# First attention: single-precision probabilities and values, one product for each head

## The reference, cut to what matters

```python
def _L0_xattn_ref(q, k, v, W_q, W_k, W_v, W_o, b_o):      # q: 32x128x128, k = v: 32x77x128
    H = 16; D_K = 8
    qh = jnp.einsum('bsd,hdk->hbsk', q, W_q)
    kh = jnp.einsum('bsd,hdk->hbsk', k, W_k)
    vh = jnp.einsum('bsd,hdk->hbsk', v, W_v)
    scores = jnp.einsum('hbsk,hbtk->hbst', qh, kh) / jnp.sqrt(D_K)
    attn = jax.nn.softmax(scores, axis=-1)
    out = jnp.einsum('hbst,hbtk->hbsk', attn, vh)
    out = jnp.transpose(out, (1, 2, 0, 3)).reshape(q.shape[0], q.shape[1], H * D_K)
    return out @ W_o.T + b_o
...
x = x + jnp.tanh(g_xattn[0]) * _L0_xattn_ref(_layernorm(x, axis=-1), ctx_1024, ctx_1024, ...)
```

## Time and profile before

| | |
|---|---|
| median of 3 runs | 1363.77 us (1361.43 to 1364.35) |
| profiled execution | 1359.99 us, its span 1358.2 us |
| TensorE busy / its weight loads | 1036.5 us / 814.9 us |
| VectorE / ScalarE / GpSimd busy | 874.3 / 859.2 / 889.6 us |
| mean granted clock of TensorE | 0.846 |
| first attention | about 135 to 303 us of the span, granted clock 0.50 from 137 us on |

### The profile page before, as it was taken

One profiled execution on the slowest core, in us unless ns is written; L12 is line 12 of the kernel. 1 busy time (PEld: TensorE's weight loads), 2 busy tenths in 40 slices (PEclk: granted clock), 3 DMA queues, 4 the chain that ended last, 5 costly groups with the idle time before them and its releaser, 6 DMA issues. The chain is left out here.

```text
span 1358.2 us, 36485 instructions
## 1 busy us (share of the span) xinstructions
PE 1036.5 (76%) x13317; PEld 814.9 (60%) x13317; DVE 874.3 (64%) x2471; ACT 859.2 (63%) x1791; POOL 889.6 (65%) x1065
## 2 busy tenths in 40 slices
PE   1568999967894499999999999899999920566660
PEld 1445777753552278887777778777777820355550
DVE  5788788876877766666666656566665611344445
ACT  0568899964663478888877778787777810233330
POOL 1160899964767456677788888888888976144441
PEclk9869555558996599999999999999999965888985
DMA  9993000000221001112112121211212111322215
GB/s 219 261 283 85 10 16 17 16 16 12 44 43 28 1 17 34 32 28 43 33 37 50 31 59 33 53 33 38 52 34 53 33 48 48 56 58 60 63 45 187
DMA packets 210051, 78.40 MB, mean 58 GB/s; under 512 B 149663, under 2 KB 206154, under 8 KB 209883
## 3 DMA queue, kind: packets, MB, share of 16 engines
q1 hardware_dynamic: 179467, 61.91, 21.1%
q10 hardware_dynamic: 25872, 5.56, 2.3%
q0 software_dynamic: 4544, 8.67, 2.0%
HBM read 14.15 MB, written 30.47 MB: 33 GB/s over the span
## 5 line engine op out<-in xcount | busy, mean ns | idle before, releaser
L1671 DVE TENSOR_REDUCE attention_negmax<-bank 128x2 f16<-128x410 f32 x256 | 137.7, 579 | 166.3 <-PE bank L1423 164.4
L1223 POOL TENSOR_TENSOR attention_pl_l<-attention_probs_l,attention_ph_l 128x512 f16<-128x512 f32 x128 | 148.3, 1159 | 97.3 <-ACT attention_ph_l L1552 95.6
L636 POOL TENSOR_TENSOR attention_probs_l<-attention_probs,attention_probs_h 77x512 f16<-77x512 f32 x128 | 145.3, 1152 | 52.8 <-ACT attention_probs_h L718 48.5
L1223 POOL TENSOR_TENSOR attention_pl_c<-attention_probs_c,attention_ph_c 77x512 f16<-77x512 f32 x128 | 147.8, 1154 | 0.0
L1984 POOL DMA_INDIRECT outputs<-experts_y_rows,experts_ids x78 | 77.5, 994 | 102.4 <-ACT experts_y_rows L1921 87.3
L1406 PE MATMUL bank<-layer_kv,ah 128*128 128x128 f16 x1024 | 108.7, 220 | 11.7 <-PEq L2062 11.5
L1438 PEld LDWEIGHTS bank<-identh,attention_negmax 128*128 128x128 f16 (+1 forms) x1024 | 83.3, 107 | 55.9 <-issue 0.3
L1452 PE MATMUL bank<-attention_vh_l,attention_ph_l 128*128 128x65 f16 x512 | 96.0, 195 | 18.2 <-POOL attention_pl_c L1223 18.2
L1406 PE MATMUL bank<-v1h,layer_kv 128*128 128x256 f16 (+1 forms) x512 | 106.4, 275 | 1.3 <-DVE attention_vl_c L1678 1.3
L1665 DVE SCALAR_TENSOR_TENSOR attention_tl<-bank,attention_th 128x512 f16<-128x512 f32 x128 | 87.8, 686 | 28.8 <-ACT attention_th L1543 28.7
L1552 ACT ACTIVATE attention_probs_l<-bank 128x512 f32<-128x512 f32 x128 | 76.2, 595 | 38.3 <-PE bank L1438 36.4
(11 more groups left out here) (367 smaller groups left out, 4150.1 us busy)
## 6 DMA issues: line engine op xcount, KB each, us to landing
tokens<-blank SPq DMA_DIRECT2D x1, 18360.0 KB, 71.0
experts_both<-outputs SPq DMA_DIRECT2D x8, 512.0 KB, 5.2
X<-in_x SPq DMA_DIRECT2D x4, 512.0 KB, 9.4
attention_pay<-attention_pay SPq DMA_DIRECT2D x8, 256.0 KB, 2.8
out<-X ACTq DMA_DIRECT2D x8, 256.0 KB, 4.3
attention_turned_h<-attention_heads_h SPq DMA_TRANSPOSE x96, 2.2
attention_turned_l<-attention_heads_l SPq DMA_TRANSPOSE x96, 2.4
outputs<-experts_y_rows,experts_ids POOLq DMA_INDIRECT x78
```

The source lines that it names most:

```text
L636: pool.tensor_tensor(probs_l[:, n % SLOTS], probs[:, n % 2], probs_h[:, n % SLOTS], ALU.subtract).then_inc(p_split, 1)
L1223: last = pool.tensor_tensor(low[:, g % 2], whole[:, g % 2], high[:, g % 2], ALU.subtract)
L1671: last = dve.tensor_reduce(negmax[:, g, 2 * i:2 * i + 2], score[i], AX.X, ALU.max, negate=True)
```

## The change

Probabilities stay in single precision: ScalarE takes one exponential of each unit into one of 8 single-precision buffers. GpSimd's program in attention0 is gone, with the buffers of high and low parts. Values are kept in single precision too, 9 numbers for each sample and head, written by ScalarE alone, which now releases the bank; VectorE's low half and its setting of the zeros are gone. TensorE makes one single-precision product for each head (77 x 128 stationary, 77 x 9 moving), and waits for exped in place of p_split. The sum of halves is gone: reciprocal and multiplication read the PSUM bank themselves, and TensorE waits for normed in place of totalled before it writes the bank again.

```diff
@@ project0, ScalarE
-                        last = act.activation(vals[:, one, :, 0, 0:DK0], head, ACT.Copy, scale=1.0 / WS)
-                    last.then_inc(v_hi, 1)
+                        last = act.activation(vals[:, one, :, 0:DK0], head, ACT.Copy, scale=1.0 / WS)
+                    last.then_inc(v_out, 1)
@@ project0, VectorE
-            for i, value in enumerate((1.0, 0.0)):
-                dve.memset(vals[:, :, :, i, DK0:DK0 + 1], value)
+            dve.memset(vals[:, :, :, DK0:DK0 + 1], 1.0)
...
-                    dve.wait_ge(v_hi, i * 2 + (u + 1))
-                    for c in range(CH):
...
-                        last = dve.scalar_tensor_tensor(vals[:, one, :, 1, 0:DK0], head, 1.0 / WS, vals[:, one, :, 0, 0:DK0],
-                                                        ALU.mult, ALU.subtract)
-                    last.then_inc(v_out, 1)
@@ attention0
-        probs = m.sb("probs", [C, 2, HG, S])
-        probs_h, probs_l = m.sb("probs_h", [C, SLOTS, HG, S], FP16), m.sb("probs_l", [C, SLOTS, HG, S], FP16)
+        probs = m.sb("probs", [C, SLOTS, HG, S])
...
-        mix = bank[6][:, 0:H * 2 * (DK0 + 1)].rearrange("p (h i k) -> p h i k", i=2, k=DK0 + 1)
+        mix = bank[6][:, 0:H * (DK0 + 1)].rearrange("p (h k) -> p h k", k=DK0 + 1)
...
-        @block.gpsimd
-        def _(pool):
-            for n in range(B * G):
-                pool.wait_ge(exped, n + 1)
-                if n >= SLOTS:
-                    pool.wait_ge(mixed, n - SLOTS + 1)
-                pool.tensor_tensor(probs_l[:, n % SLOTS], probs[:, n % 2], probs_h[:, n % SLOTS], ALU.subtract).then_inc(p_split, 1)
@@ attention0, TensorE
-                    pe.wait_ge(p_split, n + 1)
+                    pe.wait_ge(exped, n + 1)
                     if j == 0 and b:
-                        pe.wait_ge(totalled, b)
+                        pe.wait_ge(normed, b)
                     for i in range(HG):
                         v = HG * j + i
-                        pe.matmul(mix[:, v], probs_h[:, n % SLOTS, i], vals[:, b, v], start=True, stop=False)
-                        last = pe.matmul(mix[:, v, 0], probs_l[:, n % SLOTS, i], vals[:, b, v, 0], start=False, stop=True)
+                        last = pe.matmul(mix[:, v], probs[:, n % SLOTS, i], vals[:, b, v], start=True, stop=True)
@@ attention0, ScalarE
-                if n >= 2:
-                    act.wait_ge(p_split, n - 1)
                 if n >= SLOTS:
                     act.wait_ge(mixed, n - SLOTS + 1)
-                act.activation(probs[:, n % 2], score_t[n % 4], ACT.Exp)
-                act.activation(probs_h[:, n % SLOTS], score_t[n % 4], ACT.Exp).then_inc(exped, 1)
+                act.activation(probs[:, n % SLOTS], score_t[n % 4], ACT.Exp).then_inc(exped, 1)
@@ attention0, VectorE
-                dve.tensor_reduce(summed[:], mix.rearrange("p h i k -> p h k i"), AX.X, ALU.add).then_inc(totalled, 1)
-                dve.wait_ge(totalled, b + 1)
-                dve.reciprocal(recip[:], summed[:, :, DK0]).then_inc(inverted, 1)
+                dve.reciprocal(recip[:], mix[:, :, DK0]).then_inc(inverted, 1)
                 dve.wait_ge(inverted, b + 1)
-                dve.tensor_tensor(heads_out[:, b % 2], summed[:, :, 0:DK0], recip[:].unsqueeze(2).broadcast_to([S, H, DK0]),
+                dve.tensor_tensor(heads_out[:, b % 2], mix[:, :, 0:DK0], recip[:].unsqueeze(2).broadcast_to([S, H, DK0]),
                                   ALU.mult).then_inc(normed, 1)
```

More of the change, by code:

```diff
@@ L507, in project0 @@
         q_high, k_high = m.sb("q_high", [128, 2, CH, S], FP16), m.sb("k_high", [128, 2, CH, C], FP16)
-        q_done, q_hi, q_lo, k_done, k_hi, k_lo, v_done, v_hi, v_out, biased = (
-            m.sem(n) for n in ("q_done", "q_hi", "q_lo", "k_done", "k_hi", "k_lo", "v_done", "v_hi", "v_out", "biased"))
+        q_done, q_hi, q_lo, k_done, k_hi, k_lo, v_done, v_out, biased = (
+            m.sem(n) for n in ("q_done", "q_hi", "q_lo", "k_done", "k_hi", "k_lo", "v_done", "v_out", "biased"))
         block = m.block()
@@ L579, in _ @@
                                                  1.0 / WS, k_high[:, g % 2], ALU.mult, ALU.subtract).then_inc(k_lo, 1)
-                    dve.wait_ge(v_hi, i * 2 + (u + 1))
-                    for c in range(CH):
-                        one = bass.ds(i * (2 * CH) + (CH * u + c), 1)
-                        head = v_bank[u][:, D * c:D * c + D].rearrange("p (o h k) -> p o h k", o=1, k=DK0)
-                        last = dve.scalar_tensor_tensor(vals[:, one, :, 1, 0:DK0], head, 1.0 / WS, vals[:, one, :, 0, 0:DK0],
-                                                        ALU.mult, ALU.subtract)
-                    last.then_inc(v_out, 1)
         @block.gpsimd
@@ L603, in attention0 @@
         negmax = m.sb("negmax", [S, G, HG], FP16)
-        probs = m.sb("probs", [C, 2, HG, S])
-        probs_h, probs_l = m.sb("probs_h", [C, SLOTS, HG, S], FP16), m.sb("probs_l", [C, SLOTS, HG, S], FP16)
-        summed, recip, heads_out = m.sb("summed", [S, H, DK0 + 1]), m.sb("recip", [S, H]), m.sb("heads_out", [S, 2, H, DK0])
+        probs = m.sb("probs", [C, SLOTS, HG, S])
+        recip, heads_out = m.sb("recip", [S, H]), m.sb("heads_out", [S, 2, H, DK0])
         heads_h, heads_l = m.sb("heads_h", [S, 2, D], FP16), m.sb("heads_l", [S, 2, D], FP16)
@@ L609, in attention0 @@
         bn = m.sb("bn", [S, 2, 6])
-        (scored, maxed, shifted, exped, p_split, mixed, totalled, inverted, normed, heads_hi, heads_lo, projected, added,
-         bn_done) = (
-            m.sem(n) for n in ("scored", "maxed", "shifted", "exped", "p_split", "mixed", "totalled", "inverted", "normed",
-                               "heads_hi", "heads_lo", "projected", "added", "bn_done"))
+        (scored, maxed, shifted, exped, mixed, inverted, normed, heads_hi, heads_lo, projected, added, bn_done) = (
+            m.sem(n) for n in ("scored", "maxed", "shifted", "exped", "mixed", "inverted", "normed", "heads_hi", "heads_lo",
+                               "projected", "added", "bn_done"))
         turned_in = [m.sem(f"turned_in{u}") for u in range(2)]
@@ L2042, in flamingo @@
                 qst, kst = m.sb("qst", [128, HG, B, S], FP16), m.sb("kst", [128, HG, B, C], FP16)
-                vals = m.sb("vals", [C, B, H, 2, DK0 + 1], FP16)
+                vals = m.sb("vals", [C, B, H, DK0 + 1])
                 with Memory(nc, "rows0") as rows:
```

## The result

The changed kernel takes 1549.63 us (median of 4 runs, 1548.47 to 1550.75) against 1362.60 us; the ratio is 1.1373, 95% interval 1.1351 to 1.1394. It is 187 us slower. The span of the profiled execution grew from 1358.2 to 1546.7 us, by 188.5.

A forecast was written before the change was run, and what follows sets the result against it. TensorE was taken to bound the first attention, with only 0.57 us to spare a sample. +190.8 - 3 + 4.7 - 2.6 = +189.9 us on the median 1363.77 gave 1553.7 us, likeliest range 1520 to 1590.

The forecast's parts named there:

- Two passes a product, 0.213 us each: Mixing of values on TensorE: each single-precision product is two passes, each with its own weight load, at 0.213 us a pass.
- +190.8 us on TensorE: First attention's mixing: 1024 passes cost 218.1 us, less 27.3 for the present half-precision products, so +190.8 us.
- The clock stays at 0.50: First attention's stage: TensorE's granted clock was expected to stay at 0.50, the lower level of 1.2 GHz.
- The moved wait, +4.7 us: A sample's first mixing product waits for the normalised heads, released 0.15 us later, 31 times: +4.7 us.
- The removed work, -3 us: First attention: GpSimd's subtractions, ScalarE's second exponential and VectorE's sum of halves go, worth only TensorE's waits: -3 us (0 to -5).
- The projection, -2.6 us: Projection before the attention, without VectorE's low half: -1.6 us over eight groups and -1.0 at the barrier, together -2.6.
- Half the load price: Rival for mixing: a single-precision pass costs only 0.107 us, so +82 us and 1445 with the other terms; chance 5%.
- High clock: Rival for the attention stage: TensorE's clock rises to 2.4 GHz, +61 us, 1422 with the other terms; chance 8%.
- Faster: Rival for mixing: a single-precision product is as cheap as a half-precision one, 0.027 us, giving 1349 us; chance 3%.

The follow-up runs named there:

- cols27: The changed kernel with each single-precision mixing product moving 27 columns in place of nine; 1549.64 us (kernel before 1358.33).
- halves: The changed kernel with each head's product split into two products of 64 stationary columns; 1449.03 us (kernel before 1358.33).
- quarters: The changed kernel with each head's product split into four products of 32 stationary columns; 1366.14 us (kernel before 1325.88 on that chip).
- half_one: The changed kernel with probabilities and values in half precision, one product a head, low parts left out; 1341.26 us against 1358.33 for the kernel before, ratio 0.9856.
- two_banks_after: The changed kernel with the results of mixing in two PSUM banks in turn; 1486.75 us, stage 333.4 us.
- filler_before: The kernel before with six unused half-precision products of 384 moving columns added in each pair ahead of mixing; 1326.50 us against 1326.24, ratio 1.000.
- interleaved: The changed kernel with an unused half-precision product of 256 moving columns after each of the first 480 mixing products; 1570.63 us.
- moved_wait: The kernel before with one edit: TensorE waits for normed instead of totalled before the next sample's mixing; 1345.85 us against 1325.88, ratio 1.0148.
- old_work_kept: The changed kernel with ScalarE's second exponential and GpSimd's subtraction put back, results unused, TensorE waiting for the subtraction; 1511.32 us (kernel before 1326.24).
- two_banks_before: The kernel before with the results of mixing in two PSUM banks in turn; 1323.41 us against 1325.88, ratio 0.9977.

## Why the prediction was right

The forecast was 1553.7 us and +189.9; measured are 1549.6, +187.0 by the medians and +188.5 by the spans. By its steps:

- **Two passes a product, 0.213 us each.** 1024 records, 0.213 us apart. The product with two columns at line 254 was the right row, and that 128 columns at line 282 cost as much was the right hint: the load sets the pace (cols27, halves, quarters). The reading was shown, not only the number.
- **+190.8 us on TensorE.** 188.5, 5.89 us a sample in place of 5.96. The difference is at the head of the second row of mixing in a sample, which follows the scores at once. By starts its second pass came 0.073 us behind the first before, where the others stood 0.027 apart, so the old products cost a little more than I took; now it comes 0.181 behind, where the others stand 0.213 apart. 2.3 us less. half_one gives the check from the other side: 355.6 - 147.6 = 208 us between the types, of which some 6 are half_one's six samples at the higher clock, so 202 for 1024 x 0.213 - 512 x 0.027 = 204.
- **The clock stays at 0.50.** It did, from 136 us to the end of the stage. Of the reasons given, that a busy TensorE and busy loads don't lift it is shown (300.00 us of 300 busy at 0.50 in two_banks_after). That more to stream does is what filler_before did; but interleaved, with columns added too, stayed at 0.50, so the amount to stream as a guide for a forecast is only in part borne out.
- **The moved wait, +4.7 us.** The stop by starts was 230.99 - 230.30 = 0.69 and is 301.98 - 301.17 = 0.81: +0.12 us a sample, +3.7. The row that said so is the one with the sum's 0.44 us against the reciprocal's 0.29 (from its start to the next) and the multiplication's 0.29. Without the sum's going, the same edit costs 0.61 us (moved_wait).
- **The removed work, -3 us.** The passes' 32 x 5.89 = 188.5 and the wait's 3.7 less the stage's 187.8 leave -4.4 us for the waits that vanish and the two ends of the stage, where I had -3. But the missing work itself is worth 0.1 us in the changed kernel (old_work_kept): the waits for GpSimd go because TensorE has become the slow one. Right in sign, but it isn't the removal that earns it.
- **The projection, -2.6 us.** 1.2 us, and about all of it at the barrier (expected 1.0). The 0.2 us a group that I chose between 0 and 0.58 are not there: from the first conversion of values to the last it took 38.0 us and takes 37.9, so VectorE's low half of the values lay beside ScalarE's work.
- **Rivals.** Half the load price: wrong for this shape, but reachable by splitting the columns. High clock: no. Faster: its price needed a single pass of 0.027 us, which is what half_one is: 17 us faster, where the rival had 15.

The small misses nearly cancel, which is luck: passes -2.3, wait -1.0, vanished waits and ends -1.4, projection +1.4, before the projection -0.6, after the stage +2.5; in all -1.4 of 189.9 by the spans.

## What to carry to other kernels

A half-precision high and low pair of products with few moving columns costs little, since each load is cheap; one single-precision product in its place is two passes, each eight times as dear, and with nine columns behind it (or 27) the load is all one pays for. Before putting a price on an unfamiliar product, look in the trace for one of the same type and few columns, in setup if need be, and count its records. If single precision is wanted with a wide stationary operand, split its columns over the array's column groups: in quarters the same passes cost 1.7 us a sample in place of 6.8, and the sample went from 10.91 to 6.15. Here that is still 40 us more for the whole kernel than the half-precision pair (1366.14 against 1325.88).

## What the runs showed that I had not expected

- Column groups load side by side, also in single precision: 0.213 us for 128 columns, 0.0133 us a pass for 32 in turn over four groups.
- Starts of passes to different column groups 0.007 us apart.
- A TensorE busy for 300.00 us of 300 stood at a granted clock of 0.50 throughout (two_banks_after). With 12 products of 384 columns in each sample, which serve nothing, it was 1.00 for 157 us of the stage, at no cost in time (ratio 1.000), because there the ring of GpSimd and ScalarE sets the sample.
- GpSimd's subtraction of 1152 ns repeats after 1.11 us (never more than two in a row were seen); the 4.78 of two_banks_before come from two engines that wait for each other through two buffers. The busy time of neither shows that.
- VectorE's low part of the heads (128x128, single precision from SBUF) takes 280 to 293 ns when it meets no subtraction of GpSimd, and ends 0.15 us after GpSimd's when it does, which made it 1101 ns on average in the kernel before.
